# Gamma, beta and the gate product of a group norm moved behind the transpose, and two normalisations moved from VectorE to ScalarE

## The reference

```
O = einsum('hst,bthe->bshe', A, V).reshape(b, s, dim)          # retention output
mu, var = O.mean(-1), O.var(-1)
Y = (O - mu) / sqrt(var + 1e-3) * gn_gamma + gn_beta           # gamma, beta: one number a channel
W = relu(x @ wg_w)                                             # x is here the layer-normed input
x = x + tanh(g_xattn[0]) * (W * Y @ wo_w)
h = (x - mean(x)) / sqrt(var(x) + 1e-5)                        # into router and experts
logits = h @ router_w.T
```

## Time and profile before

| | |
|---|---|
| median of three runs | 403.8 us |
| the profiled execution | 402.7 us, its span 400.6 us |
| TensorE matmul busy | 340.5 us (85%) |
| VectorE busy | 214.3 us (54%) |
| ScalarE busy | 160.0 us (40%) |
| GpSimd busy | 98.4 us (25%) |

### The profile page before, as it was taken

How to read it: one execution, slowest core, us unless ns; L and a number is a source line. 1 busy time by engine, 2 the same in 40 slices (tenths; PEclk the granted TensorE clock), 3 DMA queues, 4 the chain that set the end, 5 groups by cost and what they waited for, 6 DMA issues and landing times.

```text
span 400.6 us, 4557 instructions
## 1 busy us (share of the span) xinstructions
PE 340.5 (85%) x1471; PEld 205.7 (51%) x1477; DVE 214.3 (54%) x509; ACT 160.0 (40%) x336; POOL 98.4 (25%) x148
## 2 busy tenths in 40 slices
PE   2999775609999838989799989997979989999997
PEld 1485564405666426545453646364453534444886
DVE  4144985601322257879626944693141349778921
ACT  2543221204333123144892877286795223333000
POOL 7103553430000256401440335044343001000000
PEclk9999997558999765999999999998999999999999
DMA  7996000134111114500000000000000000000011
GB/s 204 383 420 144 1 13 2 41 123 152 42 52 41 52 40 136 245 1 5 2 7 0 2 7 2 0 1 9 0 2 0 0 2 0 0 1 2 24 42 39
DMA packets 13879, 22.40 MB, mean 56 GB/s; under 512 B 2033, under 2 KB 11249, under 8 KB 13042
## 3 DMA queue, kind: packets, MB, share of 16 engines
q1 hardware_dynamic: 13090, 20.03, 14.7%
q0 software_dynamic: 768, 2.10, 1.6%
HBM read 15.83 MB, written 6.03 MB: 55 GB/s over the span
## 4 chain that ended last, share of the span: by engine, by line
PE 57%; DVE 20%; ACT 8%; issue 7%; POOL 4%; DMA 3%; another core or an unknown queue 1%; SPq 0%; DVEq 0%; ACTq 0%; POOLq 0%
PE bank L229 43%; DVE mx L1156 9%; ACT region L880 5%; PE bank L438 5%; PE bank L406 3%; DVE stats L951 2%; POOL x_sorted L697 2%; POOL rstd L673 2%; PE bank L242 1%; DVE x_sb L991 1%; PE bank L409 1%; DMA x_sb<-in_x_dram 1%; PE bank L452 1%; PE bank L486 1%; PE bank L236 1%
## 5 line engine op out<-in xcount | busy, mean ns | idle before, releaser
L1156 DVE TENSOR_REDUCE mx<-bank 128x2 f32<-128x512 f32 (+1 forms) x96 | 59.7, 682 | 14.1 <-PE bank L409 7.8
L880 ACT ACTIVATE region<-bank,padcol 128x512 f32<-128x512 f32 x96 | 60.9, 702 | 12.6 <-PE bank L229 11.6
L735 POOL TENSOR_SCALAR_AFFINE_SELECT region<-region 128x1024 f32<-128x1024 f32 x32 | 35.1, 1097 | 94.6 <-ACT region L880 94.2
L229 PE MATMUL bank<-xT,e_gu 128*128 128x512 f32 x128 | 57.6, 594 | 0.5 <-ACT xT L752 0.5
L229 PE MATMUL bank<-qst,kblk 128*128 128x512 f32 x96 | 46.0, 506 | 1.6 <-ACT region L880 0.7
L406 PE MATMUL bank<-kblk,qst 128*128 128x512 f32 x96 | 43.4, 475 | 1.7 <-DVE mx L1156 0.9
L229 PEld LDWEIGHTS bank<-xT,e_gu 128*128 128x128 f32 x128 | 23.3, 190 | 25.1 <-issue 24.3
L669 POOL TENSOR_SCALAR veps<-mv 128x1 f32<-128x1 f32 x40 | 11.4, 285 | 73.9 <-DVE mv L953 73.5
L752 ACT ACTIVATE xT<-bank 128x256 f32<-128x256 f32 x32 | 12.4, 387 | 42.4 <-PE bank L236 42.2
L409 PE MATMUL bank<-causb,identb 128*128 128x256 bf16 (+1 forms) x90 | 28.3, 314 | 0.0
L229 PE MATMUL bank<-e_down,region 128*128 128x256 f32 x128 | 27.8, 379 | 0.0
(11 more groups left out here) (155 smaller groups left out, 545.3 us busy)
## 6 DMA issues: line engine op xcount, KB each, us to landing
e_gu<-in_e_gu_dram SPq DMA_DIRECT2D x2, 1408.0 KB, 12.6
x_sorted<-zero SPq DMA_DIRECT2D x1, 1920.0 KB, 10.1
y_sorted<-region SPq DMA_DIRECT2D x15, 128.0 KB, 1.7
x_sb<-in_x_dram SPq DMA_DIRECT2D x4, 256.0 KB, 4.2
ctxT<-in_ctxT_dram SPq DMA_DIRECT2D x2, 512.0 KB, 7.5
e_down<-in_e_down_dram SPq DMA_DIRECT2D x1, 1024.0 KB, 14.3
region<-x_sorted SPq DMA_DIRECT2D x1, 1024.0 KB, 7.6
e_gu<-in_f_gate_dram SPq DMA_DIRECT2D x1, 1024.0 KB, 4.8
```

The lines of the kernel that those rows point to most:

```text
L229: return pe.matmul(dst, lhsT, rhs, start=first, stop=last)
L735: pool.affine_select(out=block, in_=block, compare_op=ALU.is_ge, fill=0.0, base=0, pattern=[[0, 2], [0, PER_GROUP], [1, P]], channel_multi ...
L880: taken(act.activation(dst, src.rearrange("p (h n) -> p h n", n=SEQ - mt * P), ACT.Exp, bias=padcol[:, key:key + 1], scale=float(HD) ** -0 ...
L1156: taken(dve.reduce_max(mx[:, b % 2, nt, quads, q, hg], src, AX), "sa")
```

## The change

The group norm's affine part changes its place. ScalarE writes (o - mean) * rstd as o * rstd + shift, where GpSimd makes shift = -mean * rstd with a multiplication and a negation more than before. TensorE turns this, and with channels on partitions gamma and beta are one number a partition, so that ScalarE applies them as scale and bias when it copies the turned tile from PSUM, in two halves of 128 columns, into yT (the space of att). The gate is computed with channels on partitions too (weights and data change sides; four matmuls of 128 columns), and VectorE's product max(gate, 0) * yT goes straight into actT. xn1 is also written by ScalarE, by scale and shift, instead of VectorE. GpSimd's group-norm work goes by two tiles at once; stat(4) goes by pairs too. gamma and beta are loaded as 128x2 columns, bo without a wait.

```diff
             def gate(k):
                 dst = acquire(pe, "rg", k, "main")
-                for t in range(KT):
-                    ins = mm(dst[:, 0:DIM], xT[:, t, tile_cols(HALF_ORDER[k])], wg[:, t, :], t == 0, t == KT - 1)
+                for half in range(KT):
+                    for t in range(KT):
+                        ins = mm(dst[:, tile_cols(half)], wg[:, t, tile_cols(half)], xT[:, t, tile_cols(HALF_ORDER[k])],
+                                 t == 0, t == KT - 1)
...
             def project(k):
-                pe.wait_ge(sem("wyT_taken"), k + 1)
+                pe.wait_ge(sem("rg_taken"), k + 1)
...
-                    pe.wait_ge(sem("rg_taken"), k + 1)
-                    turn_pair("wyT", k, att[:, k % 2, :], "turn")
+                    pe.wait_ge(sem("gn_y"), k + 1)
+                    turn_pair("wyT", k, o_sb[:, HALF_ORDER[k], :], "turn")
...
-            load(sp, "gamma", gamma[:, :], a["gamma"])
-            load(sp, "gamma", beta[:, :], a["beta"])
+            load(sp, "gamma", gn_cols[:, 0, :], a["gamma"])
+            load(sp, "gamma", gn_cols[:, 1, :], a["beta"])
...
-            sp.wait_ge(sem("gn_y"), TILES)
             load(sp, "bo", bo[:, :], a["bo"])
...
-            for k in range(TILES + 3):
-                if k < TILES:
-                    inverse_std(4, k, GN_EPS)
-                if k >= 3:
-                    inverse_std(1, k - 3, LN_EPS)
+            def scale_and_shift(layer, k, n, eps):
+                ks = slice(k, k + n)
+                pool.wait_ge(sem(f"mv{layer}"), k + n)
+                pool.tensor_scalar(veps[:, layer, ks], mv[:, layer, ks, 1], eps, None, ALU.add)\
+                    .then_inc(sem("veps"), 1)
+                chain[0] += 1
+                pool.wait_ge(sem("veps"), chain[0])
+                pool.tensor_tensor(out=rstd[:, layer, ks], in0=veps[:, layer, ks],
+                                   in1=power[:, :].to_broadcast([P, n]), op=ALU.pow).then_inc(sem(f"rstd{layer}"), n)
+                pool.wait_ge(sem(f"rstd{layer}"), k + n)
+                pool.tensor_tensor(out=shift[:, layer, ks], in0=mv[:, layer, ks, 0], in1=rstd[:, layer, ks],
+                                   op=ALU.mult).then_inc(sem("shifted"), 1)
+                shifts[0] += 1
+                pool.wait_ge(sem("shifted"), shifts[0])
+                pool.tensor_scalar(shift[:, layer, ks], shift[:, layer, ks], -1.0, None, ALU.mult)\
+                    .then_inc(sem(f"shift{layer}"), n)
+            scale_and_shift(4, 0, 2, GN_EPS)
+            for k in range(TILES + 1):
+                if k % 2 == 0 and k + 2 < TILES:
+                    scale_and_shift(4, k + 2, 2, GN_EPS)
+                if k >= 1:
+                    scale_and_shift(1, k - 1, 1, LN_EPS)
...
+            def normalised(layer, k, dst, src):
+                act.wait_ge(sem(f"shift{layer}"), k + 1)
+                return act.activation(dst, src, ACT.Identity, bias=shift[:, layer, k:k + 1], scale=rstd[:, layer, k:k + 1])
+            def group_norm(k):
+                rows = o_sb[:, HALF_ORDER[k], :]
+                normalised(4, k, rows, rows).then_inc(sem("gn_y"), 1)
+            loaded(act, "gamma", 2)
+            group_norm(0)
             for k in range(TILES + 3):
+                if k + 1 < TILES:
+                    group_norm(k + 1)
                 if k < TILES:
                     src = filled(act, "wyT", k)
                     if k >= 2:
-                        act.wait_ge(sem("res0_ready"), k - 1)
-                    taken(act.activation(actT[:, k % 2, :, :], src[:, 0:DIM].rearrange("p (t n) -> p t n", t=KT),
-                                         ACT.Copy), "wyT")
+                        act.wait_ge(sem("rg_taken"), k - 1)
+                    for t in range(KT):
+                        ins = act.activation(yT[:, k % 2, t, :], src[:, tile_cols(t)], ACT.Identity,
+                                             bias=gn_cols[:, 1, t:t + 1], scale=gn_cols[:, 0, t:t + 1])
+                    taken(ins, "wyT")
+                if 2 <= k < TILES + 2:
+                    tile = HALF_ORDER[k - 2]
+                    normalised(1, k - 2, xn1[:, tile, :], x_sb[:, tile, :]).then_inc(sem("xn1"), 1)
                 if k >= 3:
                     ln_turn(1, k - 3)
...
             for k in range(2):
                 stat(4, k, o_sb[:, HALF_ORDER[k], :])
...
-            for k in range(TILES + 2):
+            for k in range(TILES + 1):
+                if k % 2 == 0 and k + 2 < TILES:
+                    if k + 2 == TILES // 2:
+                        dve.wait_ge(sem("ro_taken"), 4)
+                    for later in (k + 2, k + 3):
+                        stat(4, later, o_sb[:, HALF_ORDER[later], :])
                 if k < TILES:
-                    dve.wait_ge(sem("gn_y"), k + 1)
-                    src = filled(dve, "rg", k)[:, 0:DIM]
+                    src = filled(dve, "rg", k)[:, 0:DIM].rearrange("p (t n) -> p t n", t=KT)
+                    dve.wait_ge(sem("wyT_taken"), k + 1)
                     if k >= 2:
-                        dve.wait_ge(sem("wyT_ready"), k - 1)
-                    taken(dve.scalar_tensor_tensor(out=att[:, k % 2, :], in0=src, scalar=0.0, in1=o_sb[:, HALF_ORDER[k], :],
-                                                   op0=ALU.max, op1=ALU.mult), "rg")
-                if k + 2 == TILES // 2:
-                    dve.wait_ge(sem("ro_taken"), 4)
-                if k + 2 < TILES:
-                    stat(4, k + 2, o_sb[:, HALF_ORDER[k + 2], :])
-                    gn_center(k + 2)
-                if k + 1 < TILES:
-                    gn_scale(k + 1)
-                if k >= 2:
-                    norm(1, k - 2)
-                if 1 <= k <= TILES:
+                        dve.wait_ge(sem("res0_ready"), k - 1)
+                    taken(dve.scalar_tensor_tensor(out=actT[:, k % 2, :, :], in0=src, scalar=0.0,
+                                                   in1=yT[:, k % 2, :, :], op0=ALU.max, op1=ALU.mult), "rg")
+                if k >= 1:
                     residual("res0", k - 1, 0)
                     dve.wait_ge(sem("res0_taken"), k)
                     stat(1, k - 1, x_sb[:, HALF_ORDER[k - 1], :])
```

More of the change, by code:

```diff
@@ L97, in build_program @@
         xn = sb("xn", [P, 2, DIM])
+        shift = sb("shift", [P, 5, TILES])
+        gn_cols = sb("gn_cols", [P, 2, KT])
         xT = sb("xT", [P, KT, TOKENS])
@@ L120, in build_program @@
         att = sb("att", [P, 2, DIM])
+        yT = att[:, :, :].rearrange("p s (t n) -> p s t n", t=KT)
         actT = sb("actT", [P, 2, KT, P])
@@ L677, in _ @@
                 inverse_std(0, k, LN_EPS)
-            for k in range(TILES + 3):
-                if k < TILES:
-                    inverse_std(4, k, GN_EPS)
-                if k >= 3:
-                    inverse_std(1, k - 3, LN_EPS)
+            def scale_and_shift(layer, k, n, eps):
[14 more added lines that the diff above has]
+                    .then_inc(sem(f"shift{layer}"), n)
+            shifts = [0]
+            scale_and_shift(4, 0, 2, GN_EPS)
[4 more added lines that the diff above has]
+                    scale_and_shift(1, k - 1, 1, LN_EPS)
             def clear_blocks(s):
@@ L1001, in _ @@
                .then_inc(sem("padcol_made"), 1)
[L1004 to L1015, removed]
             dve.wait_ge(sem("tanh"), 1)
@@ L1019, in _ @@
                 stat(4, k, o_sb[:, HALF_ORDER[k], :])
-            for k in range(2):
-                gn_center(k)
-            gn_scale(0)
-            for k in range(TILES + 2):
+            for k in range(TILES + 1):
[4 more added lines that the diff above has]
+                        stat(4, later, o_sb[:, HALF_ORDER[later], :])
                 if k < TILES:
-                    dve.wait_ge(sem("gn_y"), k + 1)
-                    src = filled(dve, "rg", k)[:, 0:DIM]
+                    src = filled(dve, "rg", k)[:, 0:DIM].rearrange("p (t n) -> p t n", t=KT)
+                    dve.wait_ge(sem("wyT_taken"), k + 1)
                     if k >= 2:
-                        dve.wait_ge(sem("wyT_ready"), k - 1)
-                    taken(dve.scalar_tensor_tensor(out=att[:, k % 2, :], in0=src, scalar=0.0, in1=o_sb[:, HALF_ORDER[k], :],
-                                                   op0=ALU.max, op1=ALU.mult), "rg")
-                if k + 2 == TILES // 2:
-                    dve.wait_ge(sem("ro_taken"), 4)
-                if k + 2 < TILES:
-                    stat(4, k + 2, o_sb[:, HALF_ORDER[k + 2], :])
-                    gn_center(k + 2)
-                if k + 1 < TILES:
-                    gn_scale(k + 1)
-                if k >= 2:
-                    norm(1, k - 2)
-                if 1 <= k <= TILES:
+                        dve.wait_ge(sem("res0_ready"), k - 1)
+                    taken(dve.scalar_tensor_tensor(out=actT[:, k % 2, :, :], in0=src, scalar=0.0,
+                                                   in1=yT[:, k % 2, :, :], op0=ALU.max, op1=ALU.mult), "rg")
```

(5 more changed lines are left out.)

## The result

The changed kernel is slower: 407.48 us median of four runs (406.79 to 408.59), against 403.97 (402.51 to 404.33, four runs) for the kernel before beside it; the ratio is 1.0092, 95% interval 1.0065 to 1.0119, or 3.5 us. The forecast was 401.7 with 398.8 to 405.4 around it, so it missed, and on the wrong side.

What follows compares the result with a forecast made beforehand. VectorE was taken to bound the stage up to the logits' copy. Start +1.99, two rounds -0.82, tiles 5 to 7 -2.33 and tail -0.97 sum to -2.1 us: 401.7 against the median of 403.8, range 398.8 to 405.4.

Steps and rivals of the forecast that it cites:

- Step 1 of the sum, the start: From the stage's start to the first residual statistics' aggregate, which moves from 42.81 to 44.80: +1.99 us.
- Steps 2 to 4: From the first aggregate to the logits' copy: -0.82 us up to tile 4, -2.33 for tiles 5 to 7, -0.97 after.
- Two rounds: From the first aggregate of the new x to that of tile 4: 2 x -0.41 = -0.82 us.
- tail: From tile 7's aggregate to the copy of the logits: 4.47 us instead of 5.43, -0.97.
- The stretched norm at the end: VectorE's last norm, 1.90 us long while GpSimd clears kblk (0.41 without), goes as ScalarE writes the last xn1.
- TensorE's clock falls: Rival in the stage: at half clock TensorE becomes the bound, +5 to +7 net, 407 to 409 us; chance 0.06.
- a clock under 1.0 before 60 us: Sign in the changed kernel's profile, at TensorE, that would show the forecast wrong.
- a ring of 3.0 a tile: Loop of waits through GpSimd, ScalarE and VectorE, once every two tiles: 6.03 us against 6.44 now; chance 0.52.
- GpSimd as the bound: Rival at GpSimd's two chains of a round: up to +1.3 us, 403.3 to 405.1; chance 0.22.
- ScalarE cheap: Rival at ScalarE: scale and bias operands cost little, 2 to 4.7 us gained, about 399.3; chance 0.16.
- Hidden: Rival after the stage: scatter, expert weights or routing wait for something else, so 403.8 us; chance 0.04.
- TensorE +0.05, off the path: The gate's eight matmuls of 128 columns take 0.91 us against about 0.86 for four of 256.

Runs made afterwards that it cites:

- the idle matmuls: Changed kernel with seven matmuls of 256 columns more on TensorE, results unread, four ahead of turn 0 and three behind it: 405.95 us.
- the best version: Changed kernel with gate 0 behind the retention outputs, selr and padselr copies behind ScalarE's loop, mean negated on VectorE, 72 waits on TensorE: 399.79 us; without the waits 401.47.
- the padding: 72 waits on a semaphore long passed, added to TensorE's program where it idles ahead of the experts; added alone to the changed kernel: 407.04 us.
- the gates first: Changed kernel with gates 0 to 3 ahead of TensorE's loop and selr, padselr copies behind ScalarE's loop: 405.10 us; with 72 waits more on TensorE 403.83.

## Why the prediction was wrong

**What bounds the kernel: right.** VectorE alone had set the pace; after the change it idles 4.8 of the 12.4 us of the two rounds.

**Durations: right,** within 0.05 us except the power of two columns (0.71 for 0.60, four times in the stage). (32 records in 3.74 us are 0.117 each and not 0.114, which makes the gate 0.93; nothing hangs on it.)

**Step 1 of the sum, the start: the step that failed.** It let gate 2 follow turn 0 after 0.27 us and run 0.91, and gave +1.99; measured were +5.2 (+5.5 from the stage's first statistics). It has no term for a wait of gate 2 for its bank. Within the loop none is needed, since gate k + 2 takes the bank of gate k - 2. At the loop's entry the order is another, and gate 2 takes gate 0's bank. The moved product turned an idle dependence into a closed chain: product 0 on ScalarE's halves, these on turn 0, gate 2 on product 0, turn 1 on gate 2. With gate 0 moved and all else as changed, the first aggregate lies 9.41 us behind the first statistics of the stage, where the kernel before has 7.98 and the changed one 13.48: +1.4 (1.99 forecast), so the rest of this step's working holds, near in size, once that wait is gone.

**Steps 2 to 4: right in mechanism, near in size.** Two rounds 12.41 us for 12.05 (the pair's chain on GpSimd took 1.75 us, not 1.52, which is 0.2 a round), tiles 5 to 7 6.10 for 5.99, tail 4.72 for 4.47. With the start repaired the stage is 1.8 us shorter, against 2.1 in the forecast. The stretched norm at the end is gone, as said: ScalarE's last write of xn1 (68.42) took 0.60 us beside the memset (68.32 to 70.16), and with xn1 back on VectorE the 1.90 came back.

**Rivals.** *TensorE's clock falls* had 0.06 and 407 to 409 us. The fall was seen, 0.50 in the window from 44, and with it one of the prediction's own signs of being wrong, a clock under 1.0 before 60 us. It was dismissed on a busy share near two thirds in the loop, though the prediction's 2.8 us in a ring of 3.0 a tile are over nine tenths (measured 11.66 of 12.41 us); and the idle time was at the entry, where the same paragraph had noted 1.6 us before turn 0. That the time of 407.5 fits this rival is luck in part: by the idle matmuls the clock is worth 1.3 us (1.7 in the profiles) of the 3.6 that the moved gate gives back, and the gather, of which the rival knows nothing, adds its own. The bank is the first cause. *GpSimd as the bound* (0.22) and *ScalarE cheap* (0.16) did not come about: the multiplication cost less than taken and the two operands their full price. *Hidden*: no; in the table the time follows the stage.

**"TensorE +0.05, off the path": wrong in a way the sum had no term for.** The time of the gate's extra matmuls was right. Their number was not weighed: 64 instructions more moved a fetch of instructions from 164 us into the gather, where it costs 1.1 to 1.7 us. The kernel before with nothing but 64 more (+1.5 us), and the best version with and without the padding (1.7 us), show the loss in time; the change with and without the padding does not (3.4 and 3.5 us over the kernel before). The loss in the gather is in every pair: 2.81 and 3.92 us in the kernel before, 2.70 and 4.51 in the changed one, 2.76 and 4.20 with the gates first, 2.78 and 3.88 in the best. In all nine kernels with a late gather the fetch starts 3.0 to 3.7 us behind the issue for tile 2, while the gather's packets move; in two of the five others, the padded ones with the gates first, it starts 1.4 us behind it, and in the remaining three 12 us ahead of it or 16 behind. The packets show that it is the fetch's transfer and not something else that goes with the length: in the window that holds all 96 packets of tiles 2 and 3 in the five other kernels, eight of the nine with the late gather have 93 and the changed kernel 95, and in six of the nine the next packet of the gather begins within 0.02 us of the fetch's end. That the three are the share of the one engine that carries the fetch is inferred from this, since the trace does not name the engine of a packet. The Trainium skill (Runtime: NRT & Kernel Launch, Instruction fetch mechanics) says that an engine's sequencer fetches its program in blocks of 256 instructions, 16 KiB, over a DMA queue of its own, and calls the cost mostly hidden. The trace agrees on the block (one packet of 0.02 MB, one more of them after) and on the queue (q8), but not on the cost: here it met a gather that VectorE was waiting for, and that took 3.9 to 4.5 us instead of 2.7 to 2.8.

**Stated bounds.** The range ended at 405.4 because its terms were prices of instructions. None of them could give 3 us; an order of banks and the place of a fetch did.

## What to carry to other kernels

When an edit makes the consumer of a buffer later, write out the buffers' rotation from the first acquisition, the entry of the loop included, and look for a producer that stands ahead of something the consumer needs. If such a chain closes, reorder one acquisition before anything else: here one moved call was worth 3.6 us. And count the instructions that an edit adds to a long program: after an edit like this one (64 more), compare the place of the instruction fetches with that of the gathers before the time is blamed on the change.

## What the runs showed of the hardware

- 64 instructions on TensorE that only wait for what is fulfilled cost 1.5 us (405.90 against 404.38), and 72 of them in a version whose gates already had 64 more gave back 1.3 (405.10 to 403.83): where the fetches fall counts, not the number of instructions.
- The fetch's packet takes about 7% of 16 engines over 1 us, so one engine for some 1.1 us, and the gather that it meets is 1.1 to 1.7 us longer. A fetch that starts 1.4 us behind the issue of tile 2 instead of 3.0 costs the gather nothing (2.74 and 2.76 us).
- TensorE's granted clock fell from 1.00 to 0.50 in the second of two pauses (1.93 and 1.43 us) and stayed there while TensorE was busy throughout the window from 44 to 48. With pauses of 0.57 and 1.43 us it fell too, 0.5 us behind the second, for 3.4 us; with pauses of 0.94 and 0.32 us it stayed at 1.00 to the last tiles.
- GpSimd's multiplication of one column takes 0.19 us, less than its addition of a constant (0.23), and of two columns as much; its power goes from 0.57 to 0.71 us with the second column.
- ScalarE's write with scale and bias read from SBUF takes 0.60 us for 256 columns from SBUF and 0.45 for 128 from PSUM.
